# Token attention of a four-layer kernel: compact queries and left factors, keys and bits spread by ScalarE, the residual's tail on GpSimd, a new order of turns

## The reference, cut to what matters

```python
def _L0_attn_ref(x, qkv_w, out_w, hex_w, hamming_lambda_logit, q6_w, transforms, transform_weights, ...):
    B, T, D, H, NT = (2, 256, 128, 16, 7)      # HD = 8; 32 sequences are given
    q, k, v = ...                              # x @ qkv_w.T, 16 heads of 8
    scores = sips_alpha[0] * jnp.tanh(einsum('bhid,bhjd->bhij', q, k) / sips_beta[0])
    soft_bits = jnp.tanh(x @ hex_w.T)          # 6 per token
    scores = scores + lam * (einsum('bid,bjd->bij', soft_bits, soft_bits) / 2.0)[:, None]
    hexc = jnp.tanh(x @ q6_w.T)                # 6 per token
    Mh = jnp.einsum('ht,tde->hde', softmax(transform_weights / TEMP), transforms)
    scores = scores + jnp.einsum('bid,hde,bje->bhij', hexc, Mh, hexc) / 6.0 * (sigmoid(scale_logit) * 2.0)
    scores = where(causal, scores, -inf)
    out = softmax(scores) @ v                  # heads side by side
    return out @ out_w.T

x = x + _layernorm(_L0_attn_ref(_layernorm(x), ...))
```

## Time and profile before

| | us |
|---|---|
| median of 3 runs | 4115.94 |
| lowest and highest | 4113.24, 4116.15 |
| the profiled execution: time | 4116.06 |
| the profiled execution: span from first to last instruction | 4114.3 |
| of it, token attention | 0 to about 909 |

### The profile page before, as it was taken

The page is one execution under the profiler, slowest core; times in us unless marked ns, Lnnn a source line. Parts: engine busy times, 40 slices in busy tenths (PEclk is TensorE's granted clock), DMA queues, the critical chain, the costliest instruction groups (busy, mean ns, idle before and its releaser), DMA issues. The chain is left out here.

```text
span 4114.3 us, 105164 instructions
## 1 busy us (share of the span) xinstructions
PE 3885.7 (94%) x35227; PEld 3023.7 (73%) x35481; DVE 3056.1 (74%) x7206; ACT 2668.9 (65%) x6345; POOL 1882.5 (46%) x1769
## 2 busy tenths in 40 slices
PE   8999999978999999899999899999999999999999
PEld 6777777756777775577777557777777777789998
DVE  6888888878999975699999675555556556556666
ACT  6888888867787873488888426666666666633333
POOL 4555555547777751366666343333334333311111
PEclk9999999999999999999999999999999999999999
DMA  3000000000000001000000110000000000000000
GB/s 108 1 0 0 0 0 0 0 2 22 21 19 23 19 23 28 16 14 16 14 14 16 23 28 15 1 0 0 0 0 0 0 0 0 0 5 9 9 9 10
DMA packets 68908, 48.04 MB, mean 12 GB/s; under 512 B 38216, under 2 KB 57552, under 8 KB 68688
## 3 DMA queue, kind: packets, MB, share of 16 engines
q1 hardware_dynamic: 68816, 46.82, 4.4%
HBM read 13.01 MB, written 4.19 MB: 4 GB/s over the span
## 5 line engine op out<-in xcount | busy, mean ns | idle before, releaser
L1650 ACT ACTIVATE l_probs<-l_act,l_neg_max 128x128 f32<-128x128 f32 (+1 forms) x1024 | 415.5, 425 | 274.0 <-DVE l_neg_max L1607 271.4
L383 POOL TENSOR_TENSOR t_probs<-t_probs,t_neg_max 128x512 f32<-128x512 f32 x384 | 392.3, 1042 | 394.0 <-DVE t_neg_max L444 394.0
L1587 POOL TENSOR_TENSOR l_probs<-l_probs,l_sums 128x512 f32<-128x512 f32 x384 | 391.0, 1039 | 366.1 <-DVE l_sums L1615 366.1
L1607 DVE TENSOR_REDUCE l_neg_max<-l_act 128x2 f32<-128x512 f32 (+1 forms) x384 | 247.1, 685 | 356.0 <-PE l_act L1762 163.3
L1968 ACT ACTIVATE e_hT<-e_act 128x512 f32<-128x512 f32 x256 | 152.8, 597 | 285.3 <-PE e_act L1989 285.3
L437 DVE SCALAR_TENSOR_TENSOR t_probs<-t_tanh_qk,scalars_sb,t_dve 128x512 f32<-128x512 f32 x384 | 269.6, 743 | 88.7 <-ACT t_tanh_qk L541 40.5
L541 ACT ACTIVATE t_tanh_qk<-t_act,t_inv_beta 128x512 f32<-128x512 f32 x384 | 242.8, 684 | 90.3 <-PE t_act L607 90.1
L832 POOL TENSOR_TENSOR w_swappedQ<-w_rawQ,w_table 128x512 f32<-128x512 f32 x128 | 162.1, 1288 | 261.2 <-ACT w_rawQ L1049 261.2
L2001 PEld LDWEIGHTS e_dve<-e_sb,e_hT 128*128 128x128 f32 x2048 | 268.7, 191 | 13.3 <-ACT e_hT L1968 0.2
L832 POOL TENSOR_TENSOR w_swappedK<-w_rawK,w_table 128x512 f32<-128x512 f32 x128 | 228.5, 1806 | 92.7 <-ACT w_rawK L1049 92.7
L2001 PE MATMUL e_dve<-e_sb,e_hT 128*128 128x128 f32 x2048 | 269.8, 275 | 0.0
(11 more groups left out here) (259 smaller groups left out, 10690.6 us busy)
## 6 DMA issues: line engine op xcount, KB each, us to landing
w_v_mid<-w_v SPq DMA_DIRECT2D x128, 130.0 KB, 2.3
z<-w_z_copy SPq DMA_DIRECT2D x32, 128.0 KB, 2.0
h<-z SPq DMA_DIRECT2D x32, 128.0 KB
out<-x_sb SPq DMA_DIRECT2D x32, 128.0 KB, 1.8
h<-z SPq DMA_DIRECT2D x32, 127.0 KB
wqkv_sb<-L_ffn_wqkv SPq DMA_DIRECT2D x2, 768.0 KB, 6.2
kv_up_sb<-L_attn_w_kv_up SPq DMA_DIRECT2D x1, 1024.0 KB, 8.5
e_sb<-L_ffn_w SPq DMA_DIRECT2D x1, 1024.0 KB, 5.6
```

The lines of the kernel that those rows point to most:

```text
L383: nc.gpsimd.tensor_tensor(p, p, neg_max[:, j, 0:len(gs)].unsqueeze(2) .broadcast_to((P, len(gs), P * (t + 1))), ALU.add).then_inc(shifted. ...
L1587: nc.gpsimd.tensor_tensor(p, p, sums[:, at, 0:len(hs)].unsqueeze(2) .broadcast_to((P, len(hs), P * (t + 1))), ALU.mult).then_inc(divided.s ...
L1607: nc.vector.tensor_reduce(neg_max[:, units.index(name), 0:len(hs)], to_act.bank("s" + name, back)[:, :].rearrange("p (h j) -> p h j", h=le ...
L1650: ins = nc.scalar.activation(probs[:, at % SLOTS, s * width:(s + 1) * width], bank[:, s * width:(s + 1) * width], ACT.Exp, bias=neg_max[:, ...
```

## The change

1. **Queries** are [128, 256]: the four heads of a row group lie on 32 rows, eight rows each, with no zeros (`compact`). One product and one copy of 256 columns take the place of two products each in `q0` and `q1`, with copies of 512 columns.
2. **Keys** are projected once in the same compact form, and ScalarE writes the four planes from that bank: four activations of 256 columns (Identity) whose scale is a column of `places`, 1 on the rows of plane g and 0 elsewhere.
3. **Left factors** are two planes, not four: two heads share a row group, sixteen rows each. `bits` is written twice, with tanh and a scale of `places` that keeps one half of the rows. `left` is one job and moves from VectorE's ring to ScalarE's. The score products stay as many and as wide.
4. **v** is one job of 256 columns.
5. **Residual's tail:** the subtraction, product and addition of `post_copied_scaled` are three GpSimd instructions of 128x256 behind the shifts of turn 5. ScalarE waits for the sequence before to be through with it ahead of its copy `out`.
6. **Order of turns:** `xnT` and `right` belong to `ahead`, in turns 4 and 5; `left`, `q` stand in turn 0, `k` in turn 1, `v` in turn 4. TensorE and ScalarE do `oT` behind the transposes `pT`, VectorE does its `pT` copy between the sums and the maxima of a turn.

```diff
...
-    MOMENTS, CENTER, SCALE, XNT = 1, 2, 3, 4
-    front_at = {0: ["right", "q0"], 1: ["k0", "q1"], 3: ["k1", "v0", "v1"], 4: ["left0", "left1"]}
-    dve_front = ["left0", "left1"]
+    MOMENTS, CENTER, SCALE = 1, 2, 3
+    ahead_at = {4: ["xnT"], 5: ["right"]}
+    front_at = {0: ["left", "q"], 1: ["k"], 4: ["v"]}
...
-        q = [sb(f"q{u}", [P, GROUPS, T]) for u in range(2)]
+        q = [sb(f"q{u}", [P, T]) for u in range(2)]
         k = [sb(f"k{u}", [P, GROUPS, T]) for u in range(2)]
-        left = [sb(f"left{u}", [P, GROUPS, T]) for u in range(2)]
-        bits = [sb(f"bits{u}", [P, T]) for u in range(2)]
+        left = [sb(f"left{u}", [P, GROUPS // 2, T]) for u in range(2)]
+        bits = [sb(f"bits{u}", [P, 2, T]) for u in range(2)]
...
+                def residual(done):
...
+                    pool.wait_ge(rst.sem, rst.done("yrstd", done))
+                    nc.gpsimd.tensor_tensor(norm.yn[:, :, :], y[:, :, :], each(norm.mv["y"][:, :, 0]), ALU.subtract)\
+                        .then_inc(updated.sem, 1)
+                    pool.wait_ge(updated.sem, updated.done("ydiff", done))
+                    nc.gpsimd.tensor_tensor(norm.yn[:, :, :], norm.yn[:, :, :], each(norm.rstd["y"][:, :]), ALU.mult)\
+                        .then_inc(updated.sem, 1)
+                    pool.wait_ge(updated.sem, updated.done("yn", done))
+                    nc.gpsimd.tensor_tensor(done.tiles(x), done.tiles(x), norm.yn[:, :, :], ALU.add)\
+                        .then_inc(updated.sem, 1)
...
                         if back:
-                            combine(i, back)
+                            summed(i, back)
                         j, seq = lagging(i, LAG, turns, back, done)
                         if seq:
                             job = "pT" + twins(j)[1]
                             to_dve.wait_filled(dve, job, seq)
                             nc.vector.tensor_copy(pT[:, 2 * j + 1, :], to_dve.bank(job, seq)[:, :])\
                                 .then_inc(to_dve.drained.sem, 1)
+                        if back:
+                            maxima(i, back)
...
+                    elif job == "right":
+                        to_act.wait_filled(act, job, seq)
+                        for s in range(2):
+                            ins = nc.scalar.activation(bits[u][:, s, :], to_act.bank(job, seq)[:, 0:T], ACT.Tanh,
+                                                       scale=w["places"][:, GROUPS + s:GROUPS + s + 1])
+                        ins.then_inc(to_act.drained.sem, 1)
+                    elif job == "q":
+                        taken(job, seq, q[u][:, :], T)
+                    elif job == "k":
+                        to_act.wait_filled(act, job, seq)
+                        for g in range(GROUPS):
+                            ins = nc.scalar.activation(k[u][:, g, :], to_act.bank(job, seq)[:, 0:T],
+                                                       ACT.Identity, scale=w["places"][:, g:g + 1])
+                        ins.then_inc(to_act.drained.sem, 1)
...
-                            ins = nc.tensor.matmul(to_act.bank("raw" + name, back)[:, at], q[u][far, g, tile],
+                            ins = nc.tensor.matmul(to_act.bank("raw" + name, back)[:, at], q[u][far, tile],
                                                    k[u][far, g, 0:width], start=s == 0, stop=last)
...
-                            nc.tensor.matmul(to_dve.bank("bil" + name, back)[:, at], left[u][near, g, tile],
-                                             bits[u][near, 0:width], start=s == 0, stop=False)
+                            nc.tensor.matmul(to_dve.bank("bil" + name, back)[:, at],
+                                             left[u][near, g // 2, tile], bits[u][near, g % 2, 0:width], start=s == 0, stop=False)
...
+                    elif job in ("q", "k"):
+                        ins = nc.tensor.matmul(bank[:, 0:T], w["t" + job][:, :], xnT[u][:, :],
                                                start=True, stop=True)
...
-    def grouped(weights):
-
-        out = np.zeros((GROUPS, GROUPS, ROWS, D), f32)
-        out[:, :, 0:TD] = np.roll(weights.reshape(GROUPS, GROUPS, TD, D), GROUPS // 2, axis=1)
-        return out.transpose(3, 0, 1, 2).reshape(D, GROUPS, P)
+    def compact(weights):
+
+        far = np.roll(weights.reshape(GROUPS, GROUPS, TD, D), GROUPS // 2, axis=1)
+        return far.transpose(3, 1, 0, 2).reshape(D, P)
```

More of the change, by code:

```diff
@@ L328, in token_attention @@
         dve_banks = [ctx.enter_context(nc.psum_tensor(f"t_dve{i}", [P, BANK], F32)) for i in range(RING)]
-        ahead_jobs = ["xnT"]
+        ahead_jobs = [job for jobs in ahead_at.values() for job in jobs]
         late_jobs = ["pT" + name for name in late(LAG)] + ["yT1", "o0", "o1", "oT", "out"]
@@ L440, in combine, with maxima @@
                             .then_inc(to_dve.drained.sem, 1)
+                def maxima(i, back):
                     for name in twins(i):
@@ L559, in step @@
                             nc.scalar.activation(p, p, ACT.Exp).then_inc(exped.sem, 1)
-                        for job in front_at.get(i, []) if front else []:
-                            if job not in dve_front:
-                                projected(job, front)
+                        for jobs, seq in ((ahead_at, ahead), (front_at, front)):
+                            for job in jobs.get(i, []) if seq else []:
+                                projected(job, seq)
                         if ahead and i == SCALE:
@@ L568, in step @@
                                     .then_inc(scaled.sem, 1)
-                        if ahead and i == XNT:
-                            taken("xnT", ahead, xnT[ahead.parity][:, :], T)
                         if done and i == BACK:
+                            if not done.first:
+                                act.wait_ge(updated.sem, updated.done("x", done.before()))
                             taken("out", done, y[:, :, :].rearrange("p a d -> p (a d)"), T)
@@ L672, in project @@
-                    ins.then_inc(ring.filled.sem, 1)
+                            ins = nc.tensor.matmul(bank[:, j * T:(j + 1) * T],
+                                                   bilinear[:, j].rearrange("a n s b -> a (n s b)"),
+                                                   bits[u][0:2 * BITS, 0, :], start=True, stop=True)
+                    ins.then_inc(to_act.filled.sem, 1)
                 def step(ahead, front, back, done):
```

139 lines of the change are left out of this document (62 added, 77 removed).

## The result

The changed kernel takes 4051.18 us (median of 4 runs, 4050.55 to 4055.77), the kernel before 4115.58 (4113.24 to 4116.15) beside it. The ratio is 0.9848, 95% interval [0.9836, 0.986]: faster by 64 us, where 80 were forecast (4036 us); the time lies inside the range of 3992 to 4085. The profiled execution took 4051.72 us, its span 4049.9.

What follows compares the result with a forecast made beforehand. The ring TensorE-ScalarE-VectorE bounds the step, TensorE's work its largest part. ScalarE's 22.9 us plus 1.9 of waits give 24.8 instead of 27.29; 32 x 2.49 = 80 off 4116.06 gives 4036 us, range 3992 to 4085.

Steps and rivals of the forecast that it cites:

- ScalarE becomes the longest: Per token-attention step, ScalarE's load was forecast at 22.9 us (22.3 to 23.5), against TensorE's 22.0 and VectorE's 21.3.
- ScalarE's additions: ScalarE's new projection work, 2.95 us a step with six activations at 0.37, replaces 2.1, adding 0.8 (0.2 to 1.4).
- the slack of 3.33: GpSimd's idle time before turn 0's shifts, 3.33 us, was to cover the 1.9 us of its three added instructions.
- under 1 us once: At the stage's end nothing hides GpSimd's three added instructions; the cost was put at under 1 us, once.
- In place of them comes no wait: VectorE loses the `left` copies and tail, 2.9 us a step, down to 21.3, with no wait replacing them.
- above all in turn 4: Copying `pT` ahead of the maxima frees its bank 1.2 us sooner; most of TensorE's 37.6 us wait goes, chiefly there.
- The waits left in turn 5: ScalarE keeps one wait for scores, about 0.75 us, and one for the product with v, 0.8, each step.
- The time from turn 4's tanh to the end of `xnT`: ScalarE's tanh pair, `pT`, `oT`, exponential pair and `xnT`, about 3.3 us, before TensorE can begin turn 5's scores.
- a few us less: Shorter `tq` and `tk` loads and first-step projections save a few us, set against the end of the stage.
- Late exponentials: Rival: maxima start 0.6 us later, delaying shifts and exponentials; 1.1 us more, 25.9 a step, 4071 us; chance 0.18.
- The clock: Rival: TensorE, less busy, drops its clock in every step; 0.8 us more, 25.6 a step, 4062 us; chance 0.11.
- Close-up: Rival: with three engines below 23 us, waits shrink to about 0.6; 23.5 a step, 3995 us; chance 0.12.

## Why the prediction was right, and where not

**Loads.** TensorE 22.9 against 22.0 of the forecast, VectorE 22.1 against 21.3, ScalarE 22.5 against 22.9, GpSimd 15.8 as forecast. "ScalarE becomes the longest" is wrong by the busy time (22.88 TensorE, 22.47 ScalarE), and by too little to matter; nor is ScalarE busy over 90% of a step, but 89%. What makes TensorE's load 0.9 more isn't shown. ScalarE's additions were priced well:

```profile
435.19 1.57 ACT L547 ACTIVATE t_k<-t_act,places_sb 128x256 f32<-128x256 f32 x4
436.62 1.30 ACT L569 ACTIVATE t_tanh_qk<-t_act,t_inv_beta 128x512 f32<-128x512 f32 x2
```

Four activations with a vector scale in 1.43 us from start to start, 0.36 each, where the row of the latent attention gave 0.37; 0.40 was the estimate by the Trainium skill, "ScalarE: Activation LUTs", "What ACT_TABLE_LOAD costs", and is 0.04 too much here. VectorE's load holds 0.5 of `t_center` that was not in my sum.

**GpSimd.** Its three instructions:

```profile
430.35 0.61 POOL L379 TENSOR_TENSOR t_yn<-t_y,t_ymv 128x256 f32<-128x256 f32 x1
431.05 0.61 POOL L382 TENSOR_TENSOR t_yn<-t_yn,t_yrstd 128x256 f32<-128x256 f32 x1
431.87 0.73 POOL L385 TENSOR_TENSOR x_sb<-x_sb,t_yn 128x256 f32 x1 [0.21 <-POOL t_yn L382]
432.56 2.03 POOL L400 TENSOR_TENSOR t_probs<-t_probs,t_neg_max 128x512 f32<-128x512 f32 x2
```

From 430.35 to the next shift it is 2.2, the upper end of 1.6 to 2.2, and the shifts of turn 0 follow at once: the slack of 3.33 is used up. ScalarE's exponentials of turn 1, which take these shifts, don't wait, so in a step it costs nothing, as I wrote; at the end of the stage it costs 1.1 ("under 1 us once").

**VectorE.** "In place of them comes no wait" is the step that the experiments correct most. The relief isn't a saving by itself; it is what the new order needs. The tail gives 8 us on the kernel before and 1 with the new projections, but 35 to 38 where the `pT` copy is first, with either projections. And 1.7 was not the tail's work alone: its two scalings last 0.60 where GpSimd is idle and 1.35 beside its shift (last section), so 0.7 of what VectorE was relieved of was a wait for GpSimd.

**The order.** I wrote that most of TensorE's wait for `pT` goes, "above all in turn 4". This failed: it is 45.9 us and not near nothing, and turn 4's tanh still waits 0.80. What the move did, with the other two parts in, was bring that wait down from 1.84, and with it went the slow stretches of the clock. The waits left in turn 5, 0.75 and 0.8 in the forecast, are 0.85 and 0.70: right. So ScalarE waits 2.74 and not 1.9, and the difference is turn 4's 0.80. The time from turn 4's tanh to the end of `xnT` adds up to 3.4 and not 3.3, which changes nothing.

**The sum.** 22.5 + 2.7 = 25.2 against 22.9 + 1.9 = 24.8: 0.4 us too low, of an engine 0.4 overpriced and waits 0.8 underpriced. By 32 steps this is 12 us of the 16 by which the total was off. The ends add 8, where I had set "a few us less" of the start against the end (the start is 2.8 more, the end 5.3), and 4 come back, since the first and the last steps gain more than a step in the middle.

**The rivals.** *Late exponentials*: one of them waits 0.21 for GpSimd in turn 4, behind a shift that had itself waited 1.16 for VectorE's maxima, and in the stage L587 waited 8.1 us for GpSimd:

```profile
L587 ACT ACTIVATE t_probs<-t_probs 128x512 f32<-128x512 f32 x384 | 233.5, 662 | 8.3 <-POOL t_probs L400 8.1
```

It is there, 0.21 a step and 0.7 more in the drain, where the rival took 1.1 a step (its own terms, three times 0.4, are 1.2). *The clock*: I had it fall more often with less work on TensorE. It went the other way: in after TensorE is busy 91% of a step and no step shows a slow stretch, while before, at 95% of a step at full clock (25.38 of 26.83), nine of thirty did. The Trainium skill's "TensorE: Matmul & The Clock Gate", "HAM oscillation", puts falls down to recurring idle gaps. The kernel with the maxima first agrees: its falls begin behind the longest of TensorE's waits in a step, 1.79 us. But every step of that kernel has this wait, and a third of them keep their clock; and on the kernel before with tail and order TensorE had waited 0.42 us, its longest wait in a step, at 173.93, and the granted clock is down to 0.86 in the next 4 us and then to this:

```profile
178.00:182.00 4.00, 4.00 (x73) 3.23 (x76) 1.80 (x8) 1.96 (x4) 1.80 (x3) 0.71 0.00 0
```

So neither the mean load nor the longest wait by itself tells which steps fall, and this stays open. *Close-up* (23.5 a step): with two instructions moved the kernel comes to 23.97, so most of what stood against it was two places in the order.

**Right by what?** The range held the time and the steps of 25.17 lie in the 24.3 to 25.4 of the forecast. But the prediction gave the gain to the loads, 25.5 to 22.9, and the table says that the same loads with the maxima first are worth 0.6 of the 1.85 us at full clock, and nothing in time. That the total came out within the range is in part luck: it priced `pT` first as a help, though alone it costs 28 us, and it had no term for the slow steps going away.

## What to carry to other kernels

Where three engines hand banks to each other in a ring, the price of a part is not its duration: try the parts in combination, and ask of each relief which wait ends last when it is there. Read the steps at full clock apart from those with a slow stretch: here the clock hid what one part gave and made up the whole of what another seemed to give. And read the order once more when the large change is in: here two moved instructions gave another 34 us, half of what the whole change had given.

## What the runs showed of the hardware

**A small VectorE instruction is held by GpSimd.** `t_center` reads two SBUF tensors of 128x2 and took a median of 151 ns before and 626 in after. The GpSimd row beside it:

```profile
440.23 2.03 POOL L400 TENSOR_TENSOR t_probs<-t_probs,t_neg_max 128x512 f32<-128x512 f32 x2 [1.16 <-DVE t_neg_max L469]
```

The first of the two shifts lasts 1.04, until 441.27; `t_center` ran from 440.66 to 441.29. It is so in all 28 steps from 70 to 840 us (0.621 to 0.627). With the tail on VectorE it is the same: shift at 433.35, its half ends at 434.39, `t_center` from 433.78 to 434.40. In the kernel before it stood at 419.98, and the first of its two shifts (from 418.95) ended at 419.99: it fell between the two. So it is held until GpSimd's running instruction ends. It lasts 0.62 in every kernel here with the copy first and `t_center` behind the maxima, the slower one of 4143.7 us too, and 0.15 in every kernel with the maxima first: moving the copy brought this wait about. This agrees with the Trainium skill, "SBUF — State Buffer", "Terms", by which the shared pair of ports is held for a whole instruction, and with "GPSIMD Engine Reference", "1. Specifications", that names instructions with two SBUF inputs. VectorE's sums, which read one operand from PSUM, last 1.41 for two beside a shift and without one.

The tail's two scalings in the kernel before were held too. At the stage's end, with GpSimd idle:

```profile
907.79 0.60 DVE L193 TENSOR_SCALAR t_yn<-t_y,t_ymv,t_yrstd 128x128 f32<-128x128 f32 x2 [1.09 <-POOL t_yrstd L179]
```

In a step they take 1.35, beside two shifts of GpSimd that begin at 433.84 and last 2.04. The first scaling lasts 1.09, from 434.87 to just behind the shifts' end at 435.88, the second 0.33. With the copy first and the tail still on VectorE they meet both shifts and take 1.69.

**TensorE's clock in the steps.** Steps with a granted clock of 0.94 last 0.9 to 1.6 us longer than their neighbours: 28.13 for 26.83 or 27.22 before, 27.70 or 27.80 for 26.42 with the maxima first, 27.98 for 26.44 with tail and order on the kernel before (0.4 with the tail back on VectorE, 27.05 for 26.64). They are about a third of the steps in the first and the third, two thirds in the second, and none ahead of the drain in the changed kernel, in those with one to three instructions moved and in that with the products repeated. So a part of what these kernels differ by, some 0.9 us a step with the maxima first, is the clock and not the waits of the step. What decides which kernel has such steps stays open.
